# Two-layer graph kernel with residual norms on one core: the first mask block in nine pieces, unit rows on three engines, another order of the transposed groups, aggregated variances

## The chip, the cores and the metric

One Trainium2 chip, one of its cores. The metric is the device time of one execution in microseconds. It was taken three times for the kernel before: median 489.86 us (489.72 to 491.61).

## What is computed

`x` is 4096 rows of 128 numbers in float32, `adj` a 4096 x 4096 matrix of zeros and ones in float32, with ones on its diagonal, `beta` one number, `weight` 128 x 128. Two layers follow one another, each with a residual and a row norm:

```python
norm2 = jnp.linalg.norm(x, axis=1, keepdims=True)
cos = beta[0] * (x @ x.T) / (norm2 @ norm2.T + 1e-07)
P = jax.nn.softmax(cos + (1.0 - adj) * -1000000000.0, axis=1)
x = _layernorm(x + P @ x)
x = _layernorm(x + adj @ (x @ weight))
```

`_layernorm` subtracts the mean of a row and divides by the root of its variance plus 1e-5.

## The kernel before

**Layer 1.** The 4096 rows of output go in NB = 8 blocks of 512. Within a block the 32 tiles of 128 neighbours go in NP = 16 pairs. For a pair, TensorE makes the scores (six matmuls of 512 columns, L890 to L892: each number is split in a high and a low half of 16 bits), ScalarE takes the exponential (`exp_pair`, L453), VectorE applies the mask (`mask_pair`, L667), ScalarE rounds to the high half (`split_hi`, L462), VectorE takes what is left as the low half (`split_lo`, L675), and TensorE multiplies both with the rows (`weigh`, L913 and L917, 16 matmuls). TensorE weighs pair m three pairs after its scores, in the first block four (`LAG0`). The scores have two slots in PSUM and the exponentials four in SBUF (`RING`).

**The mask.** The mask has to stand with the neighbour on the partitions, so every piece of `adj` takes two transfers: GpSimd issues a DMA that turns 32 bits into 8 and writes to `adj_bytes` in DRAM (`cast` L377, `cast_first` L380), and SyncE issues a transposing DMA from there into `adjT` in SBUF (L277, L283). A regular piece is four pairs (512 KB of bytes, read as 2 MB); `FIRST` names the small pieces at the start: four of one pair each. GpSimd issues a regular cast only when the piece two before it has come in transposed; `cast(2)` waits for the last small piece. `adjT` has room for all eight blocks, so no later cast waits for the compute. Per block SyncE also loads `xres` and `q_row` and stores `x1` (`load_xres`, `load_q_row`, `store_x1`).

**The start.** The rows must become unit rows, and these must be transposed. The 32 tiles of `x` come in four chunks of eight (`x_in`). VectorE and ScalarE share the sums of squares (`sum_squares` L547, L423), GpSimd takes the power -1/2 of each chunk (`inverse_norms` L384), and the multiplication is done by VectorE for chunks 0, 2 and 3 (`unit_rows` L559, one instruction of 1024 columns each) and by ScalarE for chunk 1 (L435). TensorE turns four tiles at a time, a group, into one PSUM bank (`turn_unit_rows`, L870; eight groups, banks 4 to 7 twice over). ScalarE takes the high half out of the bank (`uT_hi_part`, L428) and VectorE the low half (`uT_lo_part`, L565). A group g over 3 needs the bank of group g - 4, so it waits for that group's low half. Groups 0 to 3 are turned by the second pair, 4 to 7 in one go after the scores of the third (m == 2). Between them stand the turn of the norms (`q_turned`, L949, its bank is 7 too, moved away by `move_norms` L624), and the largest and smallest norm (`partition_extremes`, `extremes`, `scales`, L571 to L600), from which come the flag that the first exponential waits for and a power of two that scales `xaug`, the rows that `weigh` multiplies with (`xaug_hi` L468, `xaug_lo` L750, in five parts at pairs 0, 2, 4, 7 and 10).

**The norm of layer 1.** At pairs 3 to 14 of the next block, VectorE and ScalarE normalise the block before: `bn_stats` per tile, then `combine`, `mean_var`, `variance` (L687 to L705, seven instructions on 4 columns), a power on GpSimd (L400), and a scale and shift on ScalarE.

**Layer 2.** For each block TensorE adds up the neighbours (`aggregate`, L976), ScalarE moves the sum, TensorE multiplies with the weight (`weights`, L986), VectorE adds the row of layer 1 (L830; in the last block, which goes in two halves, L849), takes the moments (L853), and normalises (`normalise_rows`, L820). SyncE stores.

The order of the work is written out by hand, engine by engine; every engine runs its own list in order and waits on semaphores.

```python
order = [(a, t) for t in range(IT) for a in range(2)] if m == NP - 1 else \
    [(a, t) for a in range(2) for t in range(IT)]
```

## Time and profile before

| what | value |
| --- | --- |
| median of three runs | 489.86 us |
| lowest, highest | 489.72, 491.61 us |
| the profiled execution's own time | 491.9 us |
| its span in the profile | 490.1 us |
| TensorE busy | 466.5 us, 95% |
| VectorE busy | 376.5 us, 77% |
| ScalarE busy | 319.5 us, 65% |
| GpSimd busy | 52.7 us, 11% |
| mean granted TensorE clock | 0.993 of full |

All times inside the execution are counted from the start of the span. The profiled execution's own time holds 1.8 us that lie outside the span. The scores and weights of layer 1 take the time to 365 us, layer 2 the rest. In the rows, PE is TensorE, PEld its weight load, DVE VectorE, ACT ScalarE, POOL GpSimd, SP SyncE. A duration of an instruction includes its way through the engine's pipeline, so the distance between the starts of two neighbours on one engine is shorter than it.

### The profile page before, as it was taken

The numbers are of one execution on the slowest core, as the hardware profiler recorded it, in microseconds if no ns is written. First come the engines' busy times: TensorE is split into PE (matmuls) and PEld (weight loads), VectorE is DVE, ScalarE is ACT, GpSimd is POOL, SyncE is SP. The second block draws the span as 40 slices with busy tenths as digits, with TensorE's granted clock in tenths as the row PEclk, the third lists the DMA queues.
The fourth block names the chain that finished last, engine by engine and source line by source line (L and its number), as shares of the span: only waits on it lengthen the run. The fifth ranks groups of instructions, "written<-read, shape, count | busy, mean of one in ns | idle before, by whom it ended". The sixth has DMA issues, their size and how long they took to land.

```text
span 490.1 us, 8879 instructions
## 1 busy us (share of the span) xinstructions
PE 466.5 (95%) x3491; PEld 303.6 (62%) x3491; DVE 376.5 (77%) x623; ACT 319.5 (65%) x374; POOL 52.7 (11%) x65
## 2 busy tenths in 40 slices
PE   0988999999999999999999999999989999999994
PEld 0555667667666767677676676676664455555484
DVE  4978999999999999999999999999963022211253
ACT  5887988898898889889888988987961000000000
POOL 5310010210020120111102002000100000000011
PEclk9998999999999999999999999999999999999998
DMA  8989999999999999999998997960052010011111
GB/s 193 109 93 123 124 114 132 121 152 167 107 152 111 154 149 117 158 139 80 141 125 119 150 121 123 92 143 22 0 173 86 1 43 23 22 44 43 44 43 44
DMA packets 102250, 50.20 MB, mean 102 GB/s; under 512 B 70448, under 2 KB 98768, under 8 KB 102224
## 3 DMA queue, kind: packets, MB, share of 16 engines
q0 software_dynamic: 18480, 16.78, 41.7%
q1 hardware_dynamic: 83456, 33.06, 32.1%
q8 instruction: 11, 0.18, 0.1%
q14 instruction: 15, 0.12, 0.1%
q10 hardware_dynamic: 288, 0.07, 0.1%
HBM read 77.40 MB, written 22.82 MB: 204 GB/s over the span
## 4 chain that ended last, share of the span: by engine, by line
PE 83%; DMA 8%; DVE 3%; issue 2%; ACT 1%; POOL 1%; POOLq 0%; DVEq 0%; ACTq 0%
PE psum L976 22%; PE psum L913 20%; PE psum L917 11%; PE psum L892 10%; PE psum L890 10%; PE psum L891 10%; DMA adjT<-adj_bytes 4%; DMA adj_bytes<-in_adj 3%; PE psum L986 1%; DVE E L667 1%; DVE el L675 1%; DMA adjT<-in_x 1%; POOL rn L384 1%; ACT eh L462 1%; ACT E L453 1%
## 5 line engine op out<-in xcount | busy, mean ns | idle before, releaser
L913 PE MATMUL psum<-xaug,eh 128*128 128x257 f16 x1024 | 185.0, 274 | 3.9 <-DVE el L675 3.7
L453 ACT ACTIVATE E<-psum,sc 128x1024 f32<-128x1024 f32 x128 | 154.3, 1206 | 38.3 <-PE psum L892 37.3
L917 PE MATMUL psum<-xaug,el 128*128 128x129 f16 x1024 | 176.0, 221 | 0.0
L667 DVE SCALAR_TENSOR_TENSOR E<-E,adjT 128x1024 f32<-128x1024 f32 x128 | 155.8, 1217 | 12.6 <-ACT E L453 6.4
L675 DVE SCALAR_TENSOR_TENSOR el<-E,eh 128x1024 f16<-128x1024 f32 x128 | 155.6, 1216 | 0.0
L462 ACT ACTIVATE eh<-E 128x1024 f16<-128x1024 f32 x128 | 134.4, 1050 | 7.2 <-DVE E L667 6.8
L913 PEld LDWEIGHTS psum<-xaug,eh 128*128 128x128 f16 x1024 | 99.5, 98 | 30.3 <-DVE el L675 6.2
L976 PE MATMUL psum<-adjT,uT 128*128 128x512 fp8e4 (+1 forms) x576 | 112.1, 355 | 0.0
L917 PEld LDWEIGHTS psum<-xaug,el 128*128 128x128 f16 x1024 | 100.5, 98 | 14.0 <-issue 0.3
L890 PE MATMUL psum<-uT 128*128 (+1 forms) x256 | 98.4, 384 | 1.1 <-ACT E L453 1.1
L891 PE MATMUL psum<-uT 128*128 (+1 forms) x256 | 98.3, 384 | 0.0
L892 PE MATMUL psum<-uT 128*128 (+1 forms) x256 | 98.2, 384 | 0.0
L976 PEld LDWEIGHTS psum<-adjT,uT 128*128 128x128 f16 x576 | 56.5, 98 | 52.9
L531 ACT ACTIVATE E<-psum 128x512 f32<-128x512 f32 x7 | 4.2, 597 | 88.2 <-PE psum L976 88.2
L830 DVE TENSOR_TENSOR E<-psum,E 128x512 f32<-128x512 f32 x7 | 4.8, 691 | 68.4 <-PE psum L986 68.4
L400 POOL TENSOR_TENSOR rstd<-rstd,half_pow 128x4 f32<-128x4 f32 (+1 forms) x17 | 23.1, 1356 | 255.2 <-DVE rstd L705 255.2
L892 PEld LDWEIGHTS psum<-uT 128*128 128x128 f16 x256 | 25.3, 99 | 31.1 <-issue 1.4
L377 POOL DMA_DIRECT2D adj_bytes<-in_adj x31 | 19.5, 630 | 173.1 <-DMA adjT<-adj_bytes 173.1
L890 PEld LDWEIGHTS psum<-uT 128*128 128x128 f16 x256 | 25.3, 99 | 19.6 <-DVE uT L565 1.5
L891 PEld LDWEIGHTS psum<-uT 128*128 128x128 f16 x256 | 25.3, 99 | 16.5 <-issue 0.8
L488 ACT ACTIVATE x<-o_all,shift,rstd 128x128 f32<-128x128 f32 x32 | 14.5, 483 | 6.6 <-DVE shift L734 6.6
L820 DVE TENSOR_SCALAR E<-E,mean,rstd 128x128 f32<-128x128 f32 x32 | 9.0, 343 | 9.5 <-POOL rstd L400 9.5
(73 smaller groups left out, 159.6 us busy)
## 6 DMA issues: line engine op xcount, KB each, us to landing
adj_bytes<-in_adj POOLq DMA_DIRECT2D x31, 512.0 KB, 11.9
adjT<-in_x SPq DMA_DIRECT2D x4, 512.0 KB, 6.9
xres<-in_x SPq DMA_DIRECT2D x8, 256.0 KB, 3.3
q_row<-norms SPq DMA_DIRECT2D x8, 256.0 KB, 8.2
x_rows<-x SPq DMA_DIRECT2D x8, 256.0 KB, 2.8
E<-x_rows SPq DMA_DIRECT2D x8, 256.0 KB, 2.9
out<-E SPq DMA_DIRECT2D x16, 128.0 KB, 2.2
x_parts<-x1p SPq DMA_DIRECT2D x7, 256.0 KB, 3.6
```

What stands on the lines that cost most here:

```text
L377: pool.dma_start(piece(adj8_v, b, c), piece(adj_v, b, c)).then_inc(piece_cast[c], 16)
L400: nc.gpsimd.tensor_tensor(rstd[:, o:o + n], rstd[:, o:o + n], half_pow[:, 0:n], ALU.pow).then_inc(rstd_done, 1)
L453: nc.scalar.activation(E[:, m % RING, :, :], S[m % 2], ACT.Exp, bias=col(C_BB), scale=col(C_BS)).then_inc(e_done, 1)
L462: nc.scalar.activation(eh[:, m % RING, :, :], E[:, m % RING, :, :], ACT.Copy, scale=ECAST).then_inc(hi_done, 1)
L667: nc.vector.scalar_tensor_tensor(out=e, in0=e, scalar=EPRE, in1=mask_bytes(b, m), op0=ALU.mult, op1=ALU.min).then_inc(masked, 1)
L675: nc.vector.scalar_tensor_tensor(out=el[:, s, :, :], in0=E[:, s, :, :], scalar=ECAST, in1=eh[:, s, :, :], op0=ALU.mult, op1=ALU.subtract). ...
L890: nc.tensor.matmul(o, hj, hi, start=True, stop=False)
L891: nc.tensor.matmul(o, hj, li, start=False, stop=False)
L892: last = nc.tensor.matmul(o, lj, hi, start=False, stop=True)
L913: return nc.tensor.matmul(O[t][:, 0:XC], eh[:, s, a, cols], xaug[:, j, :], start=start, stop=stop)
L917: return nc.tensor.matmul(O[t][:, 0:D + 1], el[:, s, a, cols], xaug[:, j, 0:D + 1], start=False, stop=False)
L976: last = nc.tensor.matmul(out, x1p_all[:, j, part * D:(part + 1) * D], adj_cols(r, j, cols), start=j == 0 and part == 0, stop=j == NT - 1 ...
```

## The change

It does five things.

1. `FIRST` becomes nine pieces (1, 1, 2, 2, 2, 2, 2, 2 and 2 pairs) that make up the whole first block, and the three regular pieces of it go. From the fifth on, GpSimd issues a small cast only when the small piece three before it has come in; the first two casts of the second block wait for the seventh and eighth small piece.
2. The first chunk of `x` is loaded in two halves, the first with a semaphore of its own (`x_head`). GpSimd takes each power before the next cast instead of after two, and makes the unit rows of chunk 3 (`unit_rows_p`, eight instructions of 128 columns), in place of one of VectorE's of 1024.
3. The groups are turned in the order `TURN`: 0, 1, 2, 4, 5, 3, 6, 7. Groups 4 and 5 go after the scores of the second pair, 3, 6 and 7 after those of the third. The turn of the extremes moves in between the scores of pair 0, and VectorE takes the flag first and the rest of the scaling later.
4. The seven small instructions of a norm become one `bn_aggr` per tile and one `tensor_scalar`.
5. In the second half of the last block TensorE adds the row of layer 1 itself (`add_rows`, an identity matmul that accumulates in PSUM), and VectorE takes moments and normalises straight from PSUM.

```diff
-    FIRST = [(0, 1), (1, 1), (2, 1), (3, 1)]
+    FIRST = [(0, 1), (1, 1), (2, 2), (4, 2), (6, 2), (8, 2), (10, 2), (12, 2), (14, 2)]
...
+        TURN = (0, 1, 2, 4, 5, 3, 6, 7)
...
+            for f, (k, n) in enumerate(FIRST):
+                sp.wait_ge(first_cast[f], 16)
+                sp.dma_start_transpose(adjT[:, 0, k:k + n, :],
+                                       first_piece(adj8_v, f).bitcast(U16)).then_inc(first_in[f], 16)
+                if f == 3:
+                    sp.wait_ge(q_moved, 1)
+                    sp.dma_start(q_v, q_T[:, :]).then_inc(q_stored, 16)
...
-                if k == 2:
-                    pool.wait_ge(first_in[len(FIRST) - 1], 16)
-                elif k > 2:
-                    pool.wait_ge(piece_in[(k - 2) % MP], pieces_in(*divmod(k - 2, MP)))
+                if k < MP + 2:
+                    pool.wait_ge(first_in[len(FIRST) - 3 + k - MP], 16)
+                else:
+                    pool.wait_ge(piece_in[(k - 2) % MP], 16 * ((k - 2) // MP))
...
             def cast_first(f):
+
+                if f > 3:
+                    pool.wait_ge(first_in[f - 3], 16)
...
+            def unit_rows_p(c):
+                pool.wait_ge(rn_done, c + 1)
+                for t in range(c * CT, (c + 1) * CT):
+                    last = nc.gpsimd.tensor_scalar(work[:, t, :], xfull[:, t, :], rn[:, t:t + 1], USC, ALU.mult, ALU.mult)
+                last.then_inc(u_done_p, 1)
...
             cast_first(0)
             inverse_norms(0)
             cast_first(1)
+            inverse_norms(1)
             cast_first(2)
-            inverse_norms(1)
-            cast_first(3)
             inverse_norms(2)
             inverse_norms(3)
-            for k in range(1, 2 * MP + 2):
+            cast_first(3)
+            unit_rows_p(NC - 1)
+            for f in range(4, len(FIRST)):
+                cast_first(f)
+            for k in range(MP, 2 * MP + 2):
...
-            scales()
             unit_rows(2)
+            tiny_norms()
+            small = dve.value_load(flag[0:1, 0:1], min_val=0, max_val=1)
             uT_lo_part(1)
+            scale_step(1)
             dve.wait_ge(rn_done, NC)
             nc.vector.reciprocal(q[:, :], rn[:, :]).then_inc(norms, 1)
-            unit_rows(3)
-            small = dve.value_load(flag[0:1, 0:1], min_val=0, max_val=1)
+            scale_step(2)
+            scale_step(3)
+            scale_step(4)
...
                     if m == 1:
-                        uT_lo_part(3)
+                        uT_lo_part(4)
+                        uT_lo_part(5)
                     if m > 0:
                         split_lo(0, m - 1)
                     if m == 1:
-                        for g in range(4, UG):
-                            uT_lo_part(g)
+                        uT_lo_part(3)
+                        uT_lo_part(6)
+                        uT_lo_part(7)
...
+            def mean_var(o, n=IT, order=chain):
+                for t in range(o, o + n):
+                    last = nc.vector.bn_aggr(mv[:, t, :], stats[:, t, :])
+                last.then_inc(order, 1)
...
+                def src(t):
+                    return st[:, t, D:2 * D] if t < HT else C_last[t - HT][:, 0:D]
...
                 if g > 3:
-                    pe.wait_ge(uT_lo, g - 3)
+                    pe.wait_ge(uT_lo, TURN.index(g - 4) + 1)
...
                 if m == 1:
                     pe.wait_ge(norms, 1)
                     nc.tensor.transpose(q_turned, q[:, :], ident[:, :]).then_inc(q_filled, 1)
+                    turn_unit_rows(4)
+                    turn_unit_rows(5)
+                if m == 2:
                     pe.wait_ge(q_moved, 1)
                     turn_unit_rows(3)
-                if m == 2:
-                    for g in range(4, UG):
-                        turn_unit_rows(g)
+                    turn_unit_rows(6)
+                    turn_unit_rows(7)
...
+            def add_rows(ts):
+
+                pe.wait_ge(x1_in[1], 8 * NB)
+                for t in ts:
+                    nc.tensor.matmul(C_last[t - HT][:, 0:D], ident[:, :], stage[:, 1, t, 0:D], start=True, stop=False)
```

VectorE around the first masks, before. L667 is a mask, L565 a low half of a group, L675 a low half of a pair's exponentials, L750 a part of `xaug`, L624 the move of the norms:

```order
L667 SCALAR_TENSOR_TENSOR E<-E,adjT 128x1024
L624 COPY q_T<-psum 32x128
L565 TENSOR_TENSOR uT<-psum,uT 128x2x2x128
L750 SCALAR_TENSOR_TENSOR xaug<-adjT,sc,xaug 128x4x128
L667 SCALAR_TENSOR_TENSOR E<-E,adjT 128x1024
L565 TENSOR_TENSOR uT<-psum,uT 128x2x2x128
L675 SCALAR_TENSOR_TENSOR el<-E,eh 128x1024
L565 TENSOR_TENSOR uT<-psum,uT 128x2x2x128 x4
L667 SCALAR_TENSOR_TENSOR E<-E,adjT 128x1024
```

The same stretch of VectorE in the change, where the mask is L708, the group's low half L599, the pair's low half L716:

```order
L708 SCALAR_TENSOR_TENSOR E<-E,adjT 128x1024
L665 COPY q_T<-psum 32x128
L599 TENSOR_TENSOR uT<-psum,uT 128x2x2x128
L778 SCALAR_TENSOR_TENSOR xaug<-adjT,sc,xaug 128x4x128
L708 SCALAR_TENSOR_TENSOR E<-E,adjT 128x1024
L599 TENSOR_TENSOR uT<-psum,uT 128x2x2x128 x2
L716 SCALAR_TENSOR_TENSOR el<-E,eh 128x1024
L599 TENSOR_TENSOR uT<-psum,uT 128x2x2x128 x3
L708 SCALAR_TENSOR_TENSOR E<-E,adjT 128x1024
```

Ahead of the second pair's mask nothing differs. Behind it two groups (4 and 5) stand before the pair's low half where one (3) stood, and group 3 stands behind it, with 6 and 7.

TensorE after the scores of the second pair, before (L949 turns the norms, L870 the groups, L890 to L892 are scores):

```order
L949 MATMUL psum<-ident,q 32x128
L870 MATMUL psum<-ident,adjT 128x128 x4
L890 MATMUL psum<-uT 128x512
L891 MATMUL psum<-uT 128x512
L892 MATMUL psum<-uT 128x512
L890 MATMUL psum<-uT 128x512
L891 MATMUL psum<-uT 128x512
L892 MATMUL psum<-uT 128x512
L870 MATMUL psum<-ident,adjT 128x128 x16
```

And in the change (L991, L908, L930 to L932):

```order
L991 MATMUL psum<-ident,q 32x128
L908 MATMUL psum<-ident,adjT 128x128 x8
L930 MATMUL psum<-uT 128x512
L931 MATMUL psum<-uT 128x512
L932 MATMUL psum<-uT 128x512
L930 MATMUL psum<-uT 128x512
L931 MATMUL psum<-uT 128x512
L932 MATMUL psum<-uT 128x512
L908 MATMUL psum<-ident,adjT 128x128 x12
```

One group stood ahead of the third pair's scores and four behind them; now two (4, 5) stand ahead and three (3, 6, 7) behind, the last of which needs the bank of group 3.

GpSimd from its first cast on, before (L380 and L377 are casts, L384 the powers):

```order
L380 DMA adj_bytes<-in_adj 512x256
L384 TENSOR_TENSOR rn<-n,half_pow 128x8
L380 DMA adj_bytes<-in_adj 512x256 x2
L384 TENSOR_TENSOR rn<-n,half_pow 128x8
L380 DMA adj_bytes<-in_adj 512x256
L384 TENSOR_TENSOR rn<-n,half_pow 128x8 x2
L377 DMA adj_bytes<-in_adj 512x1024 x9
```

And in the change (L391 and L385 casts, L395 powers, L401 the unit rows):

```order
L391 DMA adj_bytes<-in_adj 512x256
L395 TENSOR_TENSOR rn<-n,half_pow 128x8
L391 DMA adj_bytes<-in_adj 512x256
L395 TENSOR_TENSOR rn<-n,half_pow 128x8
L391 DMA adj_bytes<-in_adj 512x512
L395 TENSOR_TENSOR rn<-n,half_pow 128x8 x2
L391 DMA adj_bytes<-in_adj 512x512
L401 TENSOR_SCALAR adjT<-adjT,rn 128x128 x8
L391 DMA adj_bytes<-in_adj 512x512 x5
L385 DMA adj_bytes<-in_adj 512x1024 x6
```

The eight instructions of unit rows stand between the fourth and the fifth small cast.

## Rows read from the trace of the kernel before

**Rows 1.** Stretches: us, then each engine's busy time, clock, DMA share, GB/s.
```profile
116.00:158.00 42.00, 42.00 (x353) 29.19 (x352) 40.50 (x52) 36.57 (x40) 4.47 (x5) 1.00 1.09 139
```

**Rows 2.** The chain that ended last, in time: start, us, what.
```profile
56.05 0.28 PE psum L913
```

**Rows 3.** VectorE's timeline, 21 to 35 us: start, us, instructions, [idle before].
```profile
21.53 1.21 DVE L667 SCALAR_TENSOR_TENSOR E<-E,adjT 128x1024 f32<-128x1024 f32 x1
...
22.67 0.72 DVE L565 TENSOR_TENSOR uT<-psum,uT 128x512 f16<-128x512 f32 x1
...
24.42 2.55 DVE L565 TENSOR_TENSOR uT<-psum,uT 128x512 f16<-128x512 f32 x4
...
34.61 1.22 DVE L667 SCALAR_TENSOR_TENSOR E<-E,adjT 128x1024 f32<-128x1024 f32 x1 [2.46 <-DMA adjT<-adj_bytes]
```

**Rows 4.** ScalarE's timeline, 22 to 26 us.
```profile
22.81 2.54 ACT L428 ACTIVATE uT<-psum 128x512 f16<-128x512 f32 x4
...
25.17 1.21 ACT L453 ACTIVATE E<-psum,sc 128x1024 f32<-128x1024 f32 x1
```

**Rows 5.** TensorE's timeline, 22 to 39 us.
```profile
22.17 2.00 PE L870 MATMUL psum<-ident,adjT 128*128 128x128 f32 x16
...
26.53 0.38 PE L890 MATMUL psum<-uT 128*128 128x512 f16 x1 [1.07 <-ACT E L453]
...
27.82 0.27 PE L913 MATMUL psum<-xaug,eh 128*128 128x257 f16 x1
...
30.46 0.27 PE L913 MATMUL psum<-xaug,eh 128*128 128x257 f16 x1
...
38.22 0.29 PE L913 MATMUL psum<-xaug,eh 128*128 128x257 f16 x1 [2.32 <-DVE el L675]
```

**Rows 6.** Stretches of 2 us as in rows 1: granted clock and DMA share.
```profile
26.00:28.00 2.00, 1.47 (x9) 0.78 (x10) 2.00 (x3) 2.00 (x4) 0.62 (x1) 1.00 0.05 13
...
40.00:42.00 2.00, 2.00 (x6) 0.73 (x5) 2.00 (x3) 2.00 (x3) 0.00 (x0) 0.50 1.11 103
```

**Rows 7.** GpSimd's timeline at the start, in layer 1, and in layer 2.
```profile
0.74 0.20 POOL L362 MEMSET ident<- 128x128 f32 x1 [0.29 <-POOLq L1022]
...
12.81 3.28 POOL L384 TENSOR_TENSOR rn<-n,half_pow 128x8 f32<-128x8 f32 x2
...
345.06 1.94 POOL L400 TENSOR_TENSOR rstd<-rstd,half_pow 128x4 f32<-128x4 f32 x1 [38.94 <-DVE rstd L705]
...
474.82 1.01 POOL L400 TENSOR_TENSOR rstd<-rstd,half_pow 128x4 f32<-128x4 f32 x1 [3.62 <-DVE rstd L705]
```

**Rows 8.** The lines of the small casts and their transposes, L380 and L277.
```profile
DMA to landing us min/median/max: 5.1/5.6/5.8
...
DMA to landing us min/median/max: 4.3/6.0/8.8
```

**Rows 9.** The lines of the regular casts and their transposes, L377 and L283.
```profile
DMA to landing us min/median/max: 8.9/11.9/15.3
...
DMA to landing us min/median/max: 4.1/7.1/9.8
```

**Rows 10.** Timeline of all engines, 344 to 345 us: a norm's small instructions.
```profile
344.12 0.16 DVE L687 TENSOR_TENSOR tmp<-stats 128x4 f32<-128x4 f32 x1
...
344.89 1.22 DVE L667 SCALAR_TENSOR_TENSOR E<-E,adjT 128x1024 f32<-128x1024 f32 x1
```

**Rows 11.** Timeline of all engines, 483 to 487 us: the last half block.
```profile
483.44 0.74 PE L986 MATMUL psum<-w_sb,E 128*128 128x128 f32 x4 [0.47 <-ACT E L535]
...
484.22 0.42 DVE L849 TENSOR_TENSOR E<-psum,E 128x256 f32<-128x256 f32 x1 [1.40 <-PE psum L986]
484.68 0.49 DVE L853 BATCH_NORM_STATS2 stats<-E 128x6 f32<-128x128 f32 x2
485.20 0.16 DVE L687 TENSOR_TENSOR tmp<-stats 128x2 f32<-128x2 f32 x1
...
486.12 0.70 POOL L400 TENSOR_TENSOR rstd<-rstd,half_pow 128x2 f32<-128x2 f32 x1 [3.94 <-DVE rstd L705]
```

More of the change, by code:

```diff
@@ L156, in resnorm_graph_kernel @@
         u_done_a = sem("u_done_a")
+        u_done_p = sem("u_done_p")
         uT_filled = sem("uT_filled")
@@ L235, in resnorm_graph_kernel @@
         LAG0 = LAG + 1
-        SQ_V = (5, 4, 4, 4)
+        SQ_V = [(0, 1, 4, 5, 6)] + [range(c * CT, c * CT + CT // 2) for c in range(1, NC)]
+        SQ_A = [(2, 3, 7)] + [range(c * CT + CT // 2, (c + 1) * CT) for c in range(1, NC)]
+        TURN = (0, 1, 2, 4, 5, 3, 6, 7)
         def chunk(c):
@@ L659, in mask_pair @@
                 dve.wait_ge(e_done, n + 1)
-                if not later(b) and m < len(FIRST):
-                    dve.wait_ge(first_in[m], 16)
-                elif m == 0:
-                    dve.wait_ge(piece_in[0], 16 * b)
+                if not later(b):
+                    for f, (k, _) in enumerate(FIRST):
+                        if k == m:
+                            dve.wait_ge(first_in[f], 16)
                 elif m % (NP // MP) == 0:
-                    dve.wait_ge(piece_in[m // (NP // MP)], 16 * (b + 1))
+                    dve.wait_ge(piece_in[m // (NP // MP)], 16 * b)
                 e = E[:, m % RING, :, :]
@@ L811, in _ @@
             row_moments(b, range(IT))
+            dve.wait_ge(chain, 5 * b + 4)
             norm_stats(b)
@@ L892, in scores @@
                     last = nc.tensor.matmul(o, lj, hi, start=False, stop=True)
+                    if not later(b) and m == 0 and a == 0:
+                        turn_extremes()
                 last.then_inc(s_filled, 1)
@@ L1011, in _ @@
             aggregate(r, range(0, NT // 2), BT_half[1][:, 0:HB], slice(HB, BI))
-            weights(r, C_half[0], range(0, HT), NB)
+            weights(r, C_half, range(0, HT), NB)
             aggregate(r, range(NT // 2, NT), BT_half[1][:, 0:HB], slice(HB, BI)).then_inc(half_summed, 1)
-            weights(r, C_half[1], range(HT, IT), NB + 1)
+            add_rows(range(HT, IT))
+            pe.wait_ge(sum_moved, NB + 1)
+            for t in range(HT, IT):
+                cols = slice(HB + t % 2, BI, 2)
+                last = nc.tensor.matmul(C_last[t - HT][:, 0:D], sumT[:, r % 2, cols], w_sb[:, :],
+                                        start=False, stop=True)
+            last.then_inc(c_done, 1)
 def kernel(x, adj, L0_gnn_beta, L1_gnn_weight):
```

175 lines of the change are left out of this document (87 added, 88 removed).

## Prediction

> **What bounds the kernel now.** I read the stretches first. In the second block of layer 1 TensorE is busy for 42.00 of 42.00 us, VectorE for 40.50 [rows 1]: there TensorE sets the pace, and an edit elsewhere is worth nothing as long as it keeps VectorE under that. Then the chain in time, to find where TensorE takes over for good. Up to 56.05 us the chain runs over casts, transposes and VectorE; from there on it is TensorE's own [rows 2]. So the first question is: how much earlier does the changed kernel start the weighing that begins at 56.05? That is the one of pair 9 (counted from 0), and everything behind it shifts by the same amount. The second question is the few microseconds after TensorE's last matmul.
>
> In the timelines one sees what made pair 9 late. The first weighing starts at 27.82 and the second at 30.46, so a pair costs TensorE 2.64 us when nothing fails [rows 5]. From 27.82, nine pairs at that pitch would end at 51.6; it is 56.05. The 4.45 us between are: VectorE sat idle 2.46 us before the mask of pair 4, at 34.61, since the first regular piece had not come in [rows 3]; TensorE paid for it with 2.32 us at 38.22 [rows 5]. Soon after, the granted clock stood at 0.50, which is 1.2 GHz [rows 6]; that stretch lasted about 3.4 us (39.4 to 42.8), and half of it, 1.7 us, is lost. The rest, 0.4, is small waits. Ahead of the stall, from 26 to 28 us, the DMA engines had next to nothing to do, a share of 0.05 [rows 6]: the second regular cast waited for the last small piece.
>
> **The change, part by part.**
>
> *Nine pieces.* I price a piece from the issue of its cast to the landing of its transpose, by the medians. One pair: 5.6 + 6.0 = 11.6 us [rows 8]. Four pairs: 11.9 + 7.1 = 19.0 us [rows 9]. For two pairs no row exists; the bounds are these two, and by a straight line between them it is 14.1, which I take because the small transfers at the start had company as well. The powers stand closer now: two take 3.28 us [rows 7], and by that I put the third cast at 11.3 and the fourth at 15.3. Then the pieces come in at: the third 25.4, the fourth 29.4, the fifth (behind the unit rows, issued at 20.4) 34.5, the sixth 39.5, the seventh 43.5, the eighth 48.6, the ninth 53.6, and the second block's first, issued at 43.5 with the price of four pairs, 62.5. The masks want them (below) at 28.3, 33.5, 39.2, 45.0, 49.5, 55.3, 60 and 65. Each is there at least 2.5 us ahead. So the stall at 34.61 goes, and with it TensorE's 2.32 and, I think, the fall of the clock that came behind it.
>
> *Front end.* The halved first chunk, the closer powers and the unit rows taken from VectorE bring the first mask forward by some tenths (VectorE sheds one instruction of 1.14 us, but the mask then waits for its exponential). Not further: what follows is the turn of the norms, and it stands behind the scores of the second pair on TensorE, which run at the low pace until 18.9 us in both kernels. I therefore leave the second mask where it is, at 21.5, and book nothing.
>
> *Another order of the groups.* This one costs. On VectorE a mask takes 1.14 us (21.53 to 22.67) and a group's low half 0.64 (four in 2.55) [rows 3]; a pair's low half has the mask's form and takes the same. After the mask at 21.53 come now groups 4 and 5 (to 23.95), the pair's low half (to 25.1), and only then group 3, which is out of its bank at 25.8. TensorE's last group, 7, waits for exactly this, and the scores of pairs 3 and on are queued behind it. Before, that group was turned by 24.2 (16 turns in 2.00 us from 22.17) [rows 5]. Now: group 7 turned at 26.35, its high half 0.74 more (four take 2.54) [rows 4], and behind that on ScalarE the exponential of pair 2, at 27.1 instead of 25.17, done 1.21 later, at 28.3 [rows 4]. The scores of pair 4 wait for it (that is the 1.07 at 26.53) and take 1.29, so the first weighing starts at 29.6 instead of 27.82: 1.8 us lost.
>
> *From there.* Nine pairs at 2.64 give 53.4 for pair 9. VectorE must keep up: from 28.3 it has nine masks and nine low halves at 1.14 (20.5) and the `xaug` parts, one of 0.65 and three of 1.2 (4.25), so it is done at 53.1. TensorE wins by 0.3 us; the two are level, which is why any mask that is late by more than that shows at once. Against 56.05: **2.65 us saved**.
>
> *Variances.* In a block, the seven small instructions take 0.77 us [rows 10]. `bn_aggr` has no row. Below, a small instruction starts 0.08 after the one before; above, a `bn_stats` takes 0.21: five instructions make 0.4 to 1.0. Either lies in VectorE's 1.5 us of slack per block [rows 1]; if that were gone, 0.2 per block would count. I book 0.
>
> *The last half block.* The addition on VectorE goes, 0.46 us from 484.22 to 484.68. TensorE's extra matmuls (four, half a microsecond) lie in the 0.47 us in which it waits for ScalarE anyway; if they did not fit, they would cost up to 0.5. From the end of the moments to GpSimd it took 0.92 us, 485.20 to 486.12 [rows 11]; two `bn_aggr` and one instruction with two waits I put at 0.55. Reading from PSUM may cost 0.1. **0.75 us saved.**
>
> *GpSimd's unit rows.* Eight instructions of 128 x 128. The lower bound is a memset of that size, 0.20 us; the upper the power of four columns beside a busy VectorE, 1.94 [rows 7]. I take 0.55: twice a simple instruction, since the same power takes 1.01 us when VectorE is idle and 1.94 when it works [rows 7]. The eight then end at 20.4. TensorE needs them by 25.3 only, so up to 1.15 us each they cost nothing, and the fifth small cast behind them keeps its place.
>
> The Trainium skill (GPSIMD Engine Reference, Specifications) says the SBUF interfaces are shared with VectorE, with contention when a VectorE instruction has two SBUF inputs. By that rule the trace agrees, and the change puts these eight right beside such instructions.
>
> **The sum.** 2.65 + 0.75 = 3.4 us. Span 490.1 to 486.7, the profiled execution's own 491.9 to 488.5. The median shown, 489.86, is 2.0 below that own time; carried over, 486.5.
>
> **The rivals.**
>
> *The clock falls elsewhere.* TensorE now waits about 2 us for group 3's bank, near 24 to 26. Before the drop at 39.4 it had waited 2.32. If the clock falls here for the same 3.4 us, pairs 3 and 4 run at half pace: 1.0 to 1.7 us. For it: the idle time is nearly the same. Against: the wait at 26.53 did not do it. 487.9. Chance 0.22.
>
> *The full clock comes sooner*, since groups 0 and 1 are turned back to back and the first scores start earlier. Then the second pair's scores lose some 1.1 us: 485.4. Chance 0.13.
>
> *Nine pieces are no faster than three.* Then a piece of two pairs costs as much as one of four, 19.0. The sixth piece, issued when the third has come in at 30.3, lands at 49.3 where the mask wants it at 45.0: VectorE stands 4.3 us, of which its 0.3 us of lead are free, and the time is 490.5. It begins to cost at 16.9 us a piece; at 18 it is 488.5, which I take for this rival. For it: the engines of the DMA show a share over 1 in the steady blocks [rows 1], so they may have nothing to give. Against: the first block had stretches with a share of 0.05 [rows 6], so there was something to give. 488.5. Chance 0.17.
>
> The Trainium skill (DMA: Bandwidth & Descriptors, Anatomy of one DMA) gives every DMA of this path a fixed 2.0 us beside its bytes. Two more casts would by this rule add an estimated 4 us if they ran one after another; it speaks for this rival, and three in flight speak against.
>
> *Slower: GpSimd's unit rows are the bound.* If each takes 1.94 us, they end at 31.5. Groups 6 and 7 are turned at 32.0, the exponential of pair 2 ends at 34.0, and everything comes 5.7 us later than in my sum: 492.2. It costs from 1.15 us each, and is level with the kernel before at 1.6. Chance 0.06.
>
> **How the numbers follow.** My forecast, 486.5, has 0.42. Three runs of this kernel spread over 1.9 us; 0.5% is 2.45 us, about what can be told from no change, so "faster" begins at 487.4. Faster: 0.40 of my own case, all of the early clock, 0.09 of the falling clock, 0.02 of the late pieces: 0.64. Slower than 492.3: 0.03 of GpSimd's case and 0.02 of the late pieces: 0.05. The rest, 0.31, is within. The range from 485.0 to 489.3 takes in my case with its bounds, most of the two clock cases and the pieces at 18 us.
>
> **What would show it.** Right: no wait of VectorE for `adjT` before 56 us; TensorE idle near 24 to 26 before the last group, released by VectorE's low half; first weighing near 29.6, that of pair 9 near 53.4; GpSimd's unit rows under 1 us each; the last power about 0.8 us sooner after the last matmul. Wrong: a mask that waits for its piece, a clock of 0.50 between 25 and 33 us, or a wait of TensorE for GpSimd.

## The result, and the profile after

Beside the kernel before, run on the same chip, the changed kernel took 489.89 us in the median of 20 runs (487.87 to 495.58), the kernel before 491.25. The ratio is **0.9973, 95% interval 0.996 to 0.9986**: a gain of about 1.3 us, where the prediction had 3.4. The forecast of 486.5 had been counted from 489.86, the median of the first three runs of the kernel before; in 20 runs it is 491.25. So of the 3.4 us between 486.5 and 489.89, about 1.4 belong to the base and 2.0 to the mechanism. The profiled execution took 490.71 us, its span is 488.9 (before 490.1).

Single runs can lie 1.5% or more above the fastest of their kernel, as the 495.58 here, one of 831 us of the kernel before and three of the twelve with nine pieces alone (502 to 505 us), and the medians printed below count them, which shifts none by more than 0.3 us.

First the start of layer 2, since it splits the span in two. TensorE's timeline at the start of layer 2, changed kernel (start, us, instructions):

```profile
364.64 7.72 PE L1020 MATMUL psum<-adjT,uT 128*128 128x512 fp8e4 x35
```

Before, layer 2 began at 365.12. So layer 1 gave 0.48 us and not 2.65. From there to the end it is 124.26 us, before 124.98: 0.72, where 0.75 was booked. All that is missing is missing in layer 1. The tail of the changed kernel, all engines:

```profile
482.96 0.74 PE L1068 MATMUL psum<-w_sb,E 128*128 128x128 f32 x4
483.74 0.49 DVE L891 BATCH_NORM_STATS2 stats<-psum 128x6 f32<-128x128 f32 x2 [1.79 <-PE psum L1068]
484.27 0.25 DVE L727 BATCH_NORM_AGGREGATE mv<-stats 128x2 f32<-128x6 f32 x2
484.55 0.17 DVE L733 TENSOR_SCALAR rstd<-mv 128x2 f32<-128x2 f32 x1
484.80 0.70 POOL L420 TENSOR_TENSOR rstd<-rstd,half_pow 128x2 f32<-128x2 f32 x1 [3.49 <-DVE rstd L733]
```

The addition between the matmul and the moments [rows 11] is gone, and the way from the moments to the power is two `bn_aggr` (0.25 together) and one instruction. Counted from TensorE's last long group of layer 2 (478.83 now, 479.31 before), the power starts 5.97 us later instead of 6.81.

Now the start of layer 1. VectorE's timeline of the changed kernel, which answers to rows 3:

```profile
18.42 1.27 DVE L708 SCALAR_TENSOR_TENSOR E<-E,adjT 128x1024 f32<-128x1024 f32 x1 [0.42 <-DMA adjT<-adj_bytes]
...
68.07 1.22 DVE L708 SCALAR_TENSOR_TENSOR E<-E,adjT 128x1024 f32<-128x1024 f32 x1 [3.70 <-DMA adjT<-adj_bytes]
```

These are its only two waits for a piece of the mask up to 75 us. The 2.46 us at 34.61 are gone, as forecast. In their place stand 3.70 us at 68.07, for the first piece of the second block. The kernel before had waited for the same piece, with the same mask, which the prediction did not look at. Its VectorE, and the issue of that piece's cast by GpSimd:

```profile
68.44 1.23 DVE L667 SCALAR_TENSOR_TENSOR E<-E,adjT 128x1024 f32<-128x1024 f32 x1 [1.10 <-DMA adjT<-adj_bytes]
48.08 0.61 POOL L377 DMA_DIRECT2D adj_bytes<-in_adj  x1 [12.66 <-DMA adjT<-adj_bytes]
```

So before, VectorE was ready for this mask at 67.34 and had to wait; the piece came in about 0.1 us ahead of 68.44. The change made VectorE ready 3.0 us sooner, at 64.37, and issued the cast 5.9 us sooner, at 42.16, but the piece came just 0.4 us sooner.

TensorE's timeline says what it made of that; it answers to rows 5:

```profile
25.70 0.68 PE L908 MATMUL psum<-ident,adjT 128*128 128x128 f32 x4 [2.83 <-DVE uT L599]
...
30.44 0.27 PE L955 MATMUL psum<-xaug,eh 128*128 128x257 f16 x1
...
70.48 0.29 PE L955 MATMUL psum<-xaug,eh 128*128 128x257 f16 x1 [1.66 <-DVE el L716]
```

The 2.83 us are the wait for group 3's bank, at the place and from the engine that the prediction named. The first weighing starts at 30.44, not 29.6. The stretches show why (columns as in rows 6, the clock third from the end):

```profile
24.00:26.00 2.00, 0.30 (x3) 0.34 (x4) 2.00 (x3) 0.38 (x1) 0.00 (x0) 1.00 1.24 117
26.00:28.00 2.00, 2.00 (x8) 0.87 (x7) 0.90 (x2) 1.58 (x2) 0.00 (x0) 0.53 1.23 146
28.00:30.00 2.00, 2.00 (x7) 0.67 (x6) 1.76 (x2) 2.00 (x4) 0.61 (x1) 0.61 1.26 127
```

After 0.30 us of work in two, the granted clock went to 0.50 (1.2 GHz) for about 3.4 us. Pair 9 is weighed at 54.16, 1.89 us ahead of the 56.05 of [rows 2]; then TensorE's 1.66 at 70.48 take nearly all of that back. The chain around it, in order of time (start, us, what):

```profile
42.16 11.53 DMA adj_bytes<-in_adj
53.69 0.02 issue
53.71 14.27 DMA adjT<-adj_bytes
67.97 0.03 issue
```

Cast and transpose of four pairs took 25.8 us, where the medians [rows 9] had given 19.0. Right ahead of it in the same queue, the ninth small transpose (L292, issued 45.64) did no better; the median of the nine small ones is 5.8 us:

```profile
DMA to landing us min/median/max: 13.0/13.0/13.0
```

The DMA queues of the changed kernel in 48 to 58 us and then in 60 to 64 (packets, MB, share of 16 engines):

```profile
q0 software_dynamic: 818, 0.81, 86.2%
q1 hardware_dynamic: 1087, 0.31, 27.7%
```
```profile
q1 hardware_dynamic: 45, 0.03, 15.1%
q0 software_dynamic: 19, 0.02, 5.1%
```

From 48 to 58 the casts of the second block (q0) take most of the engines' time; the transposes and the row loads (q1) get about a quarter. From 60 to 64 nearly nothing moves, and still the transpose is not in: its time is not one of bytes alone.

### The profile page after: what moved, and what is told of

Read it like the earlier page. It is cut to its first block, busy times and chain, and to the rows that moved or that the text cites. A ratio compares the mean times of both kernels' runs of the same rounds, so it can differ in the third digit from the quotient of the medians.

```text
span 488.9 us, 8865 instructions
## 1 busy us (share of the span) xinstructions
PE 466.7 (95%) x3495; PEld 304.5 (62%) x3495; DVE 371.4 (76%) x583; ACT 319.4 (65%) x374; POOL 58.3 (12%) x75
## 4 chain that ended last, share of the span: by engine, by line
PE 81%; DMA 12%; POOL 2%; DVE 2%; issue 2%; ACT 1%; POOLq 0%; SPq 0%; DVEq 0%; ACTq 0%
PE psum L1020 22%; PE psum L955 19%; PE psum L959 10%; PE psum L932 9%; PE psum L930 9%; PE psum L931 9%; DMA adjT<-adj_bytes 5%; DMA adj_bytes<-in_adj 5%; POOL rn L395 1%; PE psum L1036 1%; DMA adjT<-in_x 1%; DVE E L708 1%; DVE el L716 1%; ACT eh L487 1%; ACT E L478 1%
## 5 line engine op out<-in xcount | busy, mean ns | idle before, releaser
L708 DVE SCALAR_TENSOR_TENSOR E<-E,adjT 128x1024 f32<-128x1024 f32 x128 | 156.0, 1219 | 13.3 <-ACT E L478 8.2
L716 DVE SCALAR_TENSOR_TENSOR el<-E,eh 128x1024 f16<-128x1024 f32 x128 | 155.6, 1216 | 0.0
L930 PE MATMUL psum<-uT 128*128 (+1 forms) x256 | 98.9, 386 | 0.2 <-DVE uT L599 0.2
L932 PE MATMUL psum<-uT 128*128 (+1 forms) x256 | 98.3, 384 | 0.0
L932 PEld LDWEIGHTS psum<-uT 128*128 128x128 f16 x256 | 25.4, 99 | 31.4 <-issue 1.9
L930 PEld LDWEIGHTS psum<-uT 128*128 128x128 f16 x256 | 25.3, 99 | 18.6 <-issue 1.1
L385 POOL DMA_DIRECT2D adj_bytes<-in_adj x28 | 17.6, 629 | 148.7 <-DMA adjT<-adj_bytes 148.7
L908 PE MATMUL psum<-ident,adjT 128*128 128x128 f32 x32 | 5.8, 332 | 13.2 <-DVE adjT L593 10.4
```

The source lines that it names most:

```text
L385: pool.dma_start(piece(adj8_v, b, c), piece(adj_v, b, c)).then_inc(piece_cast[c], 16)
L708: nc.vector.scalar_tensor_tensor(out=e, in0=e, scalar=EPRE, in1=mask_bytes(b, m), op0=ALU.mult, op1=ALU.min).then_inc(masked, 1)
L716: nc.vector.scalar_tensor_tensor(out=el[:, s, :, :], in0=E[:, s, :, :], scalar=ECAST, in1=eh[:, s, :, :], op0=ALU.mult, op1=ALU.subtract). ...
L930: nc.tensor.matmul(o, hj, hi, start=True, stop=False)
L932: last = nc.tensor.matmul(o, lj, hi, start=False, stop=True)
```

## The experiments

Two theories stood against each other. **Q**: the first two big casts of the second block, now both issued while small transposes are still to come, make those transposes crawl; **B**: the DMA engines are simply full, and order alters nothing. A third concerned the front: **T**, that the new order of the turned groups costs 1.8 us and a fall of the clock besides. All ratios are to the kernel before, run beside it. Its own median was between 491.06 and 492.09 us in the four groups of runs, so where versions of different groups are compared, the ratios count beside the medians.

### The fifth cast later

```diff
-  pool.wait_ge(first_in[len(FIRST) - 3 + k - MP], 16)
+  pool.wait_ge(first_in[len(FIRST) - 3 + 2 * (k - MP)], 16)
```

("Fifth cast" is `cast(5)`, the second piece of the second block; "tenth cast" is `cast(9)`, the last one ahead of the first power of layer 1.)

> Against the changed kernel (profiled: cast 4 issued 42.16 and landed 53.7, cast 5 issued 46.87 and landed 64.6, the second block's first transpose from 53.71 to 67.97, VectorE waiting 3.70 us for it and TensorE 1.66). Cast 5 now waits for the ninth piece instead of the eighth, so it should be issued near 56 instead of 46.87. Theory Q (the small transposes and the second block's first piece crawl because two big casts share their queue with them): cast 4 lands by 51, the ninth small transpose takes under 9 us instead of 13.0, the second block's first transpose is in by 64.5, VectorE's 3.70 and TensorE's 1.66 go, total 1.3 to 1.7 us less than the changed kernel, unless the piece behind cast 5 is late in turn. Theory B (the DMA engines are full from 42 us on, so the order of the transfers alters nothing): the first piece of the second block still lands at 67 to 69, VectorE still waits 3 to 4 us at 68, the total is the changed kernel's within 0.5 us, or 1 to 3 us more if cast 5 makes the next piece late.

489.86 us in the median of 12, ratio 0.9959 (0.9941 to 0.9977). The chain:

```profile
47.52 7.66 DMA adjT<-adj_bytes
55.47 10.16 DMA adj_bytes<-in_adj
```

The ninth transpose took 7.66 instead of 13.0, the second block's first piece was in at 62.3, and neither VectorE nor TensorE waited for it. That is Q; B, by which it would land at 67 to 69 again, is out. One figure of Q missed: the first big cast was expected in by 51 and took 11.8 us, to 54.3, as long as in the changed kernel. It is the transposes that crawl. But VectorE met a new wait, behind GpSimd's queue, where the tenth cast now stood waiting for its piece in front of a power:

```profile
97.41 0.16 DVE L763 SCALAR_TENSOR_TENSOR shift<-mv,rstd 128x4 f32<-128x4 f32 x1 [2.45 <-POOL rstd L420]
```

TensorE was idle for 1.08 us between 74 and 100 in this profile, and its clock was low from about 25 to 31 us, twice as long as in the changed kernel, so that the first weighing started at 31.44 instead of 30.44. The 1.66 us gained, less 1.0 and 1.08, make a loss of 0.4, and layer 2 begins at 365.06 instead of 364.64. The total did not move.

### The row loads behind the piece

```diff
+  load_mask(1, range(1))
   sp.dma_start(rows_in_twos(xres[:, :, :]), x_v[0])
   sp.wait_ge(q_stored, 16)
   load_q_row(0)
-  load_mask(1)
+  load_mask(1, range(1, MP))
```

> Against the changed kernel. The load of xres and the load of the q row now stand behind the second block's first transpose on SyncE's queue instead of ahead of it; nothing else moves. Theory Q2 (the first transpose of the second block is held by its neighbours on the queue, xres with 14.3 us and the q row with 16.7 us among them): it lands 1.5 to 3 us sooner than 67.97 and VectorE's wait of 3.70 falls to 1 to 2 us; total 0.5 to 1.5 us less. Theory B (engines full; two small loads of together a few hundred packets are not what fills them): it is issued at 53.7 again, since cast 4 lands then, and lands at 67 to 68; VectorE waits 3.3 to 3.8; total within 0.5 us of the changed kernel, or more if the second block's q row comes late.

489.76 us, 0.9991 (0.9964 to 1.0019): nothing gained that the runs can tell. In the profile the wait moved one piece forward:

```profile
61.99 1.23 DVE L709 SCALAR_TENSOR_TENSOR E<-E,adjT 128x1024 f32<-128x1024 f32 x1 [2.46 <-DMA adjT<-adj_bytes]
```
```profile
45.11 16.79 DMA adjT<-adj_bytes
```

(VectorE, then the chain.) Here it was the ninth small transpose that took 16.79 us, with no row load near it. So the neighbours on SyncE's queue are not the cause, against what I had half expected; the casts are.

### The old order of the turned groups

```diff
-  TURN = (0, 1, 2, 4, 5, 3, 6, 7)
+  TURN = (0, 1, 2, 3, 4, 5, 6, 7)
```

and the matching calls of `turn_unit_rows`, `uT_hi_part` and `uT_lo_part` as before the change.

> Against the changed kernel. The turned groups go back to the order 0 to 7 on TensorE, ScalarE and VectorE; nine pieces, unit rows and variances stay. Theory T (the changed order makes TensorE wait 2.83 us at 25.70, after which its clock is granted at 0.50 for 3.4 us): TensorE's wait there falls to about 1.1, the first weighing starts at 27.5 to 28.5 instead of 30.44, the clock stays at full between 26 and 30, the ninth pair's weighing starts near 52 instead of 54.16. What that gives at the end depends on the second block's first piece: if that still lands near 68 (theory B), TensorE's wait for it grows from 1.66 to about 3.5 and the total stays within 0.5 us; if block 0 being ahead also brings the piece sooner, the total is 1.5 to 2.5 us less. Rival: without the changed order a mask of pair 2 or 3 is wanted before its piece is in and VectorE waits for it, 0.5 to 1.5 us, and the first weighing is no sooner than 29.

488.53 us, 0.9943 (0.9917 to 0.9968). TensorE's timeline:

```profile
26.86 0.38 PE L924 MATMUL psum<-uT 128*128 128x512 f16 x1 [1.08 <-ACT E L478]
...
28.15 0.27 PE L949 MATMUL psum<-xaug,eh 128*128 128x257 f16 x1
...
62.84 0.28 PE L949 MATMUL psum<-xaug,eh 128*128 128x257 f16 x1 [1.15 <-DVE el L712]
```

First weighing at 28.15 instead of 30.44, clock at 1.00 between 20 and 50 us. Layer 2 begins at 362.26, 2.38 sooner than in the changed kernel. The new wait now hits the ninth small piece (transpose 14.29 us), not the second block's. T holds for the start of layer 1. For the total this pair of versions alone leaves it close: the two intervals just overlap (the changed kernel's is 0.996 to 0.9986).

### Nine pieces alone, on the kernel before

```diff
-  FIRST = [(0, 1), (1, 1), (2, 1), (3, 1)]
+  FIRST = [(0, 1), (1, 1), (2, 2), (4, 2), (6, 2), (8, 2), (10, 2), (12, 2), (14, 2)]
```

with the paced casts and waits of the change.

> The kernel before with only the nine paced pieces: old order of the turned groups, all unit rows as before, old variances. Theory as in the prediction: the wait of 2.46 us at 34.61 and TensorE's 2.32 at 38.22 go, the ninth pair's weighing starts at 52 to 53 instead of 56.05. If the second block's first piece comes near 68 whatever is done (theory B), VectorE waits for it 3 to 5 us and the total is 0 to 1 us less than the kernel before. If the piece comes by 65, the total is 3 to 3.5 us less.

490.24 us, 0.9979 (0.9958 to 1.0). In the profiled execution the span was 486.3, with no wait for a mask but 0.42 at the very first: layer 2 begins at 361.30, 3.8 us sooner than before, where the prediction's terms without the new order make 4.45 (2.65 and the 1.8 that it had taken off for the order). In that execution the fifth cast happened to go out at 51.96 only, since the eighth small piece came late; so it ran almost as if it had been held back. The median is just 1.1 us below the kernel before. The profile is the shortest of 12 executions: one good profile says little of the median.

### Both first casts behind the ninth piece

```diff
-  pool.wait_ge(first_in[len(FIRST) - 3 + k - MP], 16)
+  pool.wait_ge(first_in[len(FIRST) - 1], 16)
```

> The changed kernel with both first casts of the second block behind the ninth piece: the ninth small cast and its transpose have the queue to themselves. A measurement of the disputed cost. Theory Q: the ninth small transpose takes 3.5 to 6 us here, against 13.0 beside two big casts in the changed kernel and 7.66 beside one; the two casts are issued near 50 and take 14 to 18 us together, the second block's first piece comes at 73 to 76 and VectorE waits 8 to 11 us for it, the total rises by 5 to 9 us. Theory B (what fills the engines is total load, whatever its kind): the ninth transpose still takes over 9 us.

A single run: 488.85 us. Here my figures missed widely, and to the good side. The last two small transposes (L292), the two casts (L385), and the second block's first transpose (L287):

```profile
DMA to landing us min/median/max: 3.0/3.7/4.4
```
```profile
DMA to landing us min/median/max: 10.5/12.8/15.1
```
```profile
DMA to landing us min/median/max: 8.5/8.5/8.5
```

With no big cast beside them the small transposes take 3.0 and 4.4 us. Without transposes beside them, the first of two casts issued together is done in 10.5 and the second in 15.1; in the changed kernel, issued 4.7 us apart, they took 11.5 and 17.7. So the piece whose cast was issued at 47.16, five microseconds later than in the changed kernel, came in at 66.1, almost two sooner than there. I had expected 73 to 76. VectorE took that mask at 66.21:

```profile
66.21 1.23 DVE L708 SCALAR_TENSOR_TENSOR E<-E,adjT 128x1024 f32<-128x1024 f32 x1 [2.42 <-ACT E L478]
```

The row blames ScalarE's exponential. But this pair's exponential had ended at 63.6, and the piece landed 0.1 us ahead of the mask: it was the DMA. The wait is for several semaphores.

### Old order and later fifth cast; then the power ahead of the cast

The first combines the two edits (run twice). The second adds this (run twice):

```diff
-  for k in range(MP, 2 * MP + 2):
+  for k in range(MP, 2 * MP + 1):
       cast(k)
...
       power(b + 1, 0, IT)
-      for k in range((b + 2) * MP + 2, (b + 3) * MP + 2):
+      for k in range((b + 2) * MP + 1, (b + 3) * MP + 1):
```

> Against the changed kernel: the turned groups in the old order and the fifth cast behind the ninth piece, together. With the old order alone the ninth small transpose, issued at 46.04 beside two big casts, took 14.29 us, and VectorE waited 1.67 us for it at 60.43; with the fifth cast held back it took 7.66 us (with the changed order). Theory Q: it takes under 9 us here too, there is no wait for a mask in block 0 or at the second block's first pair, TensorE's clock stays full after its first start, and the second block's first weighing comes 1 to 1.5 us sooner than with the old order alone. The price: the tenth cast then waits long in GpSimd's queue ahead of the first power, which starts near 93 to 96, and VectorE waits 1.2 to 2.5 us for it (as 2.45 us at 97.41 in the run with the fifth cast held back), 0 to 1.1 us of it TensorE's. Total within 0.8 us of the old order alone, to either side. Theory B (the engines are full, only their order changes): the piece behind the fifth cast is late instead, and VectorE waits over 1 us for a mask near 76.

489.48 us, 0.9969 (0.9941 to 0.9996).

> The old order of the turned groups and the fifth cast held back, once more, with the power behind the tenth cast as in the change. Theory W: a power that waits behind a late cast is what put half of this version's runs at spans of 488.5 to 490.9; the median is 488.5 to 490 again, 1.5 us or more above that of the version with the power ahead, run beside it. Rival: those were disturbed runs of that hour, and the two medians are within 0.6 us.

488.99 us, 0.9948 (0.9919 to 0.9977).

> The kernel with the old order of the turned groups and the fifth cast held back, and in it the power of each block of layer 1 ahead of the last of its casts on GpSimd's queue instead of behind it. If the tenth cast, waiting for a piece, is what delays the power, VectorE's wait for it near 93 to 97 falls from 1.2 to 2.5 us to nothing, TensorE's idle there goes, and the total is 0.5 to 1.1 us less than without this edit; this would be the fastest version, 484.5 to 485.5 us of span at a clock of 0.998. If it is not, nothing moves there. What it may cost: the tenth cast comes up to 4 us later, so its piece, and with it a mask of the third block near 107, may be late by 0 to 2 us.

**486.70 us, 0.991 (0.9885 to 0.9935)**, 6 runs.

> The fastest version once more, unchanged, beside its version without the power's move, since its median came from 6 runs: 486.70. If that is its level, it is 486.3 to 487.3 here too, ratio to the kernel before 0.989 to 0.993. If it was a lucky six, the median is 488 to 489.5, as that of the version without the power's move (489.48 of 12 runs, six of them with spans of 484.8 to 486.7 and six of 488.5 to 490.9).

486.90 us, 0.9926 (0.9893 to 0.996), 7 runs. This version has the lowest medians of all; it beats the kernel before, and both its ratios lie below the changed kernel's 0.9973. Its first profile, TensorE's timeline:

```profile
26.02 0.38 PE L924 MATMUL psum<-uT 128*128 128x512 f16 x1 [1.06 <-ACT E L478]
...
27.31 0.27 PE L949 MATMUL psum<-xaug,eh 128*128 128x257 f16 x1
...
360.11 12.25 PE L1012 MATMUL psum<-adjT,uT 128*128 128x512 fp8e4 x56
```

From 59 us to the end of layer 1 nothing stops TensorE for more than 0.1 us in either profile but the 1.36 us that both kernels lose behind the last pair. In the second, VectorE waited 1.19 us at 74.33 for the piece of the fifth cast, as theory B has it, but TensorE had work and did not stop. In the first profile the ninth transpose and the second block's first one took this each:

```profile
DMA to landing us min/median/max: 7.6/7.6/7.6
```

What the power's move does is less clear. The wait that it removes is there in the second run without it:

```profile
93.15 0.16 DVE L759 SCALAR_TENSOR_TENSOR shift<-mv,rstd 128x4 f32<-128x4 f32 x1 [1.79 <-POOL rstd L420]
```

and there it made TensorE idle once:

```profile
95.64 0.28 PE L949 MATMUL psum<-xaug,eh 128*128 128x257 f16 x1 [0.41 <-DVE el L712]
```

In the first run without the move VectorE did not wait for the power at all. Layer 2 begins at 360.49 and 360.80 without the move and at 360.11 and 360.84 with it. Yet the medians differ by 2.8 us in the first couple and 2.1 in the second. The ratios' intervals are apart in the first couple and overlap in the second, with 6 and 7 runs of the version with the move against 12 and 12. So the times lean to theory W, but it is not shown: no profile has 2 us to give, and what made about half of the runs without the move 3 to 7 us longer than the shortest stays open.

### The power ahead, without the later cast

The edit above on the old order, with the fifth cast where the change has it.

> The old order of the turned groups and the power ahead of the tenth cast, with the fifth cast where the change has it (behind the eighth piece). It tells apart which of the fastest version's two edits on GpSimd's queue counts. Theory Q (the pace of the fifth cast): the ninth small transpose crawls again beside two big casts, 11 to 15 us, VectorE waits 1 to 2.5 us for its piece near 60, the second block's first weighing comes near 70 instead of 69.9 less that, and the median is 1 to 2 us above the fastest version's 486.70. Rival W (it was the power's place that counted): the median is within 0.6 us of 486.70.

489.35 us, 0.9954 (0.9924 to 0.9983). In the chain the ninth transpose crawls again:

```profile
46.52 13.71 DMA adjT<-adj_bytes
```

VectorE waited 2.00 us at 60.33, and layer 2 began at 362.16, against 360.11 and 360.84 with the later cast too; the median is 2.4 to 2.7 us above the fastest version's. The power's move alone brings nothing that these runs can tell from the old order alone.

### The changed order kept, all else as in the fastest

> The changed kernel with the fifth cast held back and the power ahead of the tenth cast, and with the changed order of the turned groups kept: it differs from the fastest version (span 484.4, median 486.70) by that order alone. Theory T, the order costs what the prediction booked for it and a clock fall besides: TensorE waits 2.8 to 3.9 us at 25.2 to 25.7 for VectorE's low half instead of 1.06 at 26.02, the first weighing starts near 29 instead of 27 to 27.5, the clock of most runs is 0.990 to 0.996 instead of 0.998, and the median is 1.5 to 3 us above the fastest version's, since no late piece hides it any more. Rival S, the supply of pieces hides it: the second block's first weighing is at the same time in both, and the median is within 0.8 us of 486.70.

489.58 us, 0.9972 (0.9953 to 0.9992): 2.9 and 2.7 us above the fastest version's two medians; by the ratios it is 3.0 and 2.3. TensorE:

```profile
25.49 1.09 PE L908 MATMUL psum<-ident,adjT 128*128 128x128 f32 x4 [3.55 <-DVE uT L599]
...
31.26 0.27 PE L955 MATMUL psum<-xaug,eh 128*128 128x257 f16 x1
```

Here no late piece follows, so the whole price shows: first weighing at 31.26 instead of 27.31, layer 2 at 363.63 instead of 360.11. The clock stood at 0.50 from about 25 to 31 us, one stretch of which is:

```profile
26.00:28.00 2.00, 2.00 (x7) 0.92 (x6) 0.61 (x1) 1.39 (x2) 0.00 (x0) 0.50 1.00 123
```

### Without the unit rows on GpSimd and the new variances

The kernel before with nine pieces, the later fifth cast and the power ahead.

> The kernel before with nine paced pieces, the fifth cast held back and the power ahead of the tenth cast: it differs from the fastest version by the shared unit rows and the aggregated variances with their half block alone. Theory V, these two are worth what the tail shows and no more: the last power starts 1.3 us later than in the fastest version, relative to TensorE's last turned row, and the span is 0.8 to 1.4 us above 484.4; the median 487.3 to 488.3. Rival: what made the fastest version fast is the pieces' pace alone, the median is within 0.4 us of 486.70. Other rival: without GpSimd's unit rows the first block starts later by 0.5 us or more and the clock falls, 2 us or more.

488.72 us, 0.9956 (0.9938 to 0.9973), so 2.0 and 1.8 above the fastest (by the ratios 2.3 and 1.5). In the profile 0.7 us of that are the tail: from the start of layer 2 the span runs 125.0 us, against 124.3. The rest is the front end, which I had not expected. VectorE's first mask waited for its piece:

```profile
20.35 1.23 DVE L670 SCALAR_TENSOR_TENSOR E<-E,adjT 128x1024 f32<-128x1024 f32 x1 [1.49 <-DMA adjT<-adj_bytes]
```

and the first weighing is at 29.26. On the changed front it was at 27.31 to 27.70 in five of six profiles with the old order. So theory V, the tail and no more (0.8 to 1.4), explains 0.7 of the profile's 2.7 us (487.1 against 484.4); the rest is where the other rival had it, at the first block's start, but without a fall of the clock. How large the front end's part is, is open: with the same front end, the kernel before with nine pieces alone had its first weighing at 28.17, and its first mask waited 0.42 instead of 1.49.

## Why the prediction was wrong

**What failed.** It is the sum's first term. The prediction said that everything behind pair 9 "shifts by the same amount": 2.65 us there, 2.65 at the end. Of these, 1.89 came at pair 9 and 0.48 at the end of layer 1. Two things broke it.

1. *"Nine pieces"* priced every piece by the medians of the kernel before, and the second block's first piece by "the price of four pairs", 19.0: in at 62.5, wanted at 65, spared by 2.5 us. It took 25.8 and came at 67.97. That price had been measured with other neighbours. A closer row existed: in the kernel before this same piece took 20.3 us (cast issued at 48.08) and already made VectorE wait 1.10 us, so its supply had nothing to spare there. With it the piece would still have been forecast at 63.8, in time; what no row of the kernel before shows is the price beside small transposes. The change issues one big cast ahead of the ninth small transpose (42.16, the transpose 45.64), a second right behind it (46.87), and both ahead of the big transpose. Beside two casts the ninth small transpose takes 13.0 to 16.8 us (changed kernel, old order, rows behind the piece, power ahead without the later cast), beside one 7.2 to 9.0 (the seven profiles with only the fifth cast held back), and with both casts held back, 3.0. This cost TensorE 1.66 us. It is shown: the fifth cast held back took the wait for this piece away in all seven profiles that have it.
2. *"The clock falls elsewhere"* was a rival with chance 0.22, and it happened on top: 0.8 us, at the place and at the length it named (0.50 for 3.4 us), the price under the 1.0 to 1.7 it was given. From the turn of the last group to the first weighing it took 4.74 us here, against 3.89 and 3.90 in the two profiles of this order whose clock stayed. In two others (fifth cast later; all else as in the fastest) it took 5.8, so there the fall cost 1.9. I had set it low since the wait at 26.53 had not done it. The wait here was 2.83, nearer to the 2.32 before the fall in [rows 5, 6] than to the 1.07. The rows could have given it more weight.

Together: 2.65 forecast, less 0.8, less 1.66, makes 0.2; 0.48 was measured. The 0.3 between them is not traced.

**What was right.** *"Another order of the groups"*: 1.8 us, first weighing at 29.6. Where the clock stays, it is 29.35 and 29.07 in the changed order against some 27.4 in the old, 1.7 to 2.0. But the prediction took this part as given and never asked what the kernel is without it; undoing it brought the start of layer 2 forward by 2.38 us against the changed kernel and by 3.52 where no late piece followed. With the 0.8 of the clock added, the first weighing was at 30.44 and pair 9 at 54.16, each 0.8 behind the forecast. *"GpSimd's unit rows"*: booked 0.55 each, measured:

```profile
16.39 3.88 POOL L401 TENSOR_SCALAR adjT<-adjT,rn 128x128 f32<-128x128 f32 x8
```

which is 0.485 each, done at 20.3, where 20.4 was written; the rival with 1.94 is out. The Trainium skill (GPSIMD Engine Reference, Specifications) names contention with VectorE when its instruction has two SBUF inputs, as a mask has. The traces agree, in a small size: the eight took 2.80 us in the old order alone, where VectorE sat idle for 1.20 us of that time, and 3.76 to 3.89 in the other profiles that show them. *Price of a two-pair piece*: booked 14.1; the median of the two-pair casts from the fourth on is 6.7 and that of the two-pair transposes before the ninth 5.7, together 12.4; the ninth piece took 19.1. *Variances*: 0 booked, none seen. *"The last half block"*: 0.75 booked, 0.72 to 0.84 measured. *"Nine pieces are no faster than three"* is out for the first block: it would have shown as a wait near 45, and there is none. *"The full clock comes sooner"*: not in this profile, where the first scores at the fast pace start at 19.3 us, at 19.1 before. In the other profiles of the changed order they start at 17.0 to 17.6, and TensorE then only waited longer for group 3's bank (3.5 to 3.8 us). *"Front end"*: 0 booked. That was a little too low: once the old order is back, the first weighing is 0.1 to 0.5 us sooner than before [rows 5] in five profiles and 0.3 later in one; beside the two profiles of the old front end with nine pieces (28.17 and 29.26) it is up to about 1.9 sooner.

**The signs that were named.** "No wait for `adjT` before 56 us" (beyond 0.42 at the first mask), "TensorE idle near 24 to 26" and the power were right; they watched the first block only. The list had a clock of 0.50 between 25 and 33 us as a sign of being wrong, and that is what stood there. No sign was named for the second block.

## What to carry to other kernels

A price from issue to landing belongs to its neighbours in the queue: when a change brings a transfer's start forward, price it again beside what will then be in flight, and follow the supply one block beyond the place where the engine "takes over", looking for waits of the engines that are not the bottleneck: here VectorE's 1.10 us at 68.44 stood in the profile before and cost nothing yet. When a stretch of work is made to wait, look also at what kind of wait brought the clock down elsewhere in the same profile. And try each part of a change without the others: here a helpful part (pieces, tail) and a harmful one (order of the groups) nearly cancelled, and the version with the harmful one undone, one cast paced and the power moved was 0.7 to 0.9% faster than before instead of 0.3%; without the power's move it was 0.3 to 0.5%.

## What the runs showed of the hardware

- *Starting a cast later can bring its data sooner.* A 512 KB cast and its transpose from 42.16 came in at 67.97, from 47.16 at 66.1. In flight together, the ninth transpose and the second block's first one took 13.0 and 14.3 us, with the casts held back 3.0 and 8.5; the two casts took 11.5 and 17.7 instead of 10.5 and 15.1. By what mechanism the runs don't tell; that a transpose still took four microseconds to end when the engines moved almost nothing (60 to 64 us) was measured in one profile.
- *The clock does not fall by the length of a wait alone.* With the changed order TensorE waited 2.83, 3.55 and 3.63 us for that bank and the clock fell each time; it waited 3.51 and 3.83 us at the same place in two others (both casts behind the ninth piece; rows behind the piece) and it did not:

```profile
26.00:28.00 2.00, 1.32 (x8) 0.43 (x6) 1.07 (x2) 2.00 (x3) 0.00 (x0) 1.00 0.50 87
```

  This is the stretch after the 3.51 us. The mean granted clock of an execution was 0.993 or less in 33 of 57 executions with the changed order, and in 4 of 85 with nine pieces and the old one. A mean does not say where the clock fell: the kernel before, with the old order but with its stall at 38.22, has it in 36 of 99. So with the changed order it falls far more often; what decides in a single execution is open.
- *`bn_aggr` is cheap*: two on one tile each in 0.25 us, beside two `bn_stats` in 0.49.
